# A short clear and a wait for it behind every state gather of the four layers

## The reference

```
h = jnp.maximum(_layernorm(x, axis=-1), 0.0);  x = x + L0(h, src, dst, edge_type)
h = jnp.maximum(_layernorm(x, axis=-1), 0.0);  x = x + L1(h, edge_index)
h = jnp.maximum(_layernorm(x, axis=-1), 0.0);  x = x + L2(h, src, dst)
h = jnp.maximum(_layernorm(x, axis=-1), 0.0);  x = x + L3(h, edge_index)

L0:  m = sum over r of mask[etypes == r] * (feat[src] @ weight[r]);  segment_sum(m, dst)
L1:  three times   h = segment_sum(h[src], dst) / max(cnt, 1) @ Wl + h @ Wr + b   (relu between)
L2:  f = feat * rsqrt(out_deg);  s = segment_sum(f[src], dst);  t = segment_sum(f[src] * f[dst], dst)
     (s @ weight1 + t @ weight2) * rsqrt(in_deg)
L3:  two graph attention layers (4 heads of 32, then 1 head of 64): softmax over each dst's edges
```

## Time and profile before

| | before |
|---|---|
| median of 3 runs | 6565.89 us (6560.53 to 6572.52) |
| profiled execution: its span (its own time is given by no other number) | 8635.1 us |
| mean granted TensorE clock in the profiled execution | 0.650 |
| GpSimd busy, share of the span | 4305.3 us, 50% |
| VectorE busy | 4326.1 us, 50% |
| TensorE busy (multiplications) | 4016.2 us, 47% |
| ScalarE busy | 2282.2 us, 26% |

### The profile page before, as it was taken

How to read it: one execution, slowest core, us unless ns; L and a number is a source line. 1 busy time by engine, 2 the same in 40 slices (tenths; PEclk the granted TensorE clock), 3 DMA queues, 4 the chain that set the end, 5 groups by cost and what they waited for, 6 DMA issues and landing times. The chain is left out here.

```text
span 8635.1 us, 76490 instructions
## 1 busy us (share of the span) xinstructions
PE 4016.2 (47%) x19708; PEld 2671.9 (31%) x19708; DVE 4326.1 (50%) x14882; ACT 2282.2 (26%) x5999; POOL 4305.3 (50%) x4026
## 2 busy tenths in 40 slices
PE   1111158312888825654563664342465476567000
PEld 0000034101555514443442443332344355233000
DVE  3010069301999944434432553565244698677553
ACT  0000000001777621110110333354111133799000
POOL 5777720575000046546555674774555100888577
PEclk8555589655999955555555555555666666798555
DMA  1111100000222222222222343343122144555222
GB/s 42 47 46 47 47 19 0 21 1 5 103 113 107 99 70 79 69 73 64 69 68 63 112 128 112 94 139 112 44 68 68 77 161 163 125 146 138 76 82 77
DMA packets 413612, 684.96 MB, mean 79 GB/s; under 512 B 283685, under 2 KB 290444, under 8 KB 407978
## 3 DMA queue, kind: packets, MB, share of 16 engines
q1 hardware_dynamic: 282410, 542.14, 17.7%
q0 software_dynamic: 130944, 140.05, 7.5%
HBM read 310.94 MB, written 373.78 MB: 79 GB/s over the span
## 5 line engine op out<-in xcount | busy, mean ns | idle before, releaser
L711 POOL DMA_INDIRECT G<-states,srcq x1568 | 1678.9, 1071 | 851.1 <-issue 479.5
L1133 DVE TENSOR_TENSOR_SCAN R<-same,R,G 128x28 f32<-128x28 f32 x4480 | 883.8, 265 | 622.1 <-issue 499.9
L1793 PE MATMUL PS<-ident,HH 128*128 128x128 f32 x2357 | 529.8, 376 | 1257.4 <-ACT AT L2063 373.2
L2063 ACT COPY AT<-PS 128x512 f32<-128x512 f32 (+1 forms) x494 | 283.7, 581 | 2467.3 <-remote 1375.1
L1793 PEld LDWEIGHTS PS<-ident,HH 128*128 128x128 f32 x2357 | 402.8, 205 | 1332.9 <-issue 409.9
L711 POOL DMA_INDIRECT EE<-node_info,srcq x392 | 394.4, 1006 | 545.0 <-DMA node_info<-XC 415.7
L1701 PE MATMUL PS<-R 128*128 128x392 f16 x784 | 283.0, 361 | 673.2 <-remote 375.7
L711 POOL DMA_INDIRECT G<-states,srci x392 | 406.7, 1038 | 321.0 <-ACT HH L2161 199.1
L1808 PEld LDWEIGHTS PS<-WD,AT 128*128 128x128 f32 x2358 | 505.8, 316 | 183.0 <-issue 182.7
L1808 PE MATMUL PS<-WD,AT 128*128 128x64 f32 x2358 | 560.6, 416 | 0.0
L824 POOL DMA_INDIRECT out_nodes<-O,dstq x392 | 430.9, 1099 | 188.2 <-issue 123.3
(11 more groups left out here) (412 smaller groups left out, 10157.6 us busy)
## 6 DMA issues: line engine op xcount, KB each, us to landing
states<-O SPq DMA_DIRECT2D x70, 896.0 KB, 3.6
HH<-states SPq DMA_DIRECT2D x56, 896.0 KB
total<-R SPq DMA_DIRECT2D x56, 896.0 KB
XB<-resid SPq DMA_DIRECT2D x42, 896.0 KB
states<-HH SPq DMA_DIRECT2D x28, 896.0 KB, 3.9
G<-states,srcq POOLq DMA_INDIRECT x1568
resid<-XB SPq DMA_DIRECT2D x28, 896.0 KB
xl_of_src<-O SPq DMA_DIRECT2D x14, 1792.0 KB
```

Source lines behind the costliest of these rows:

```text
L711: return pool.indirect_dma_start(to, None, table_, bass.IndirectOffsetOnAxis(ap=idx, axis=0), bounds_check=bound, oob_is_err=False).then_i ...
L1133: last = dve.tensor_tensor_scan(out=out_[:, order, f], data0=flags[:, order], data1=in_[:, order, f], initial=initial[:, f:f + 1], op0=ALU ...
L1793: last = pe.transpose(PS[:, 4 + k, q * P:(q + 1) * P], HH[:, b, (g * G4 + q) * D2:(g * G4 + q + 1) * D2], ident[:])
L2063: act.copy(AT[:, k, 0:n * P], PS[:, 4 + k, 0:n * P]).then_inc(s_copied, 1)
```

## The change

A tile `idle` of 64 columns is added, which nothing reads. Behind each gather of a layer GpSimd clears it (`memset`, 128 x 64 numbers) as a `step`: it waits for the end of the clear before it goes on. There are 4 x 14 x 28 = 1568 such pairs. The other phases' gathers stay as they were, and so do the waits for `chunk_scanned`.

```diff
@@ -148,6 +148,7 @@
         fw = sb("fw", [P, 2, 6, HCOLS])
+        idle = sb("idle", [P, 64])
@@ -713,6 +714,9 @@
+            def pause():
+                step(pool.memset(idle[:], 0.0))
+
             moved = 0
@@ -819,6 +823,8 @@
                     for j in range(C):
                         gather(G[:, b, j * D:(j + 1) * D], table_, idx[:, at + j:at + j + 1], table_.shape[0] - 1, s_g[b])
+                        if phase in LAYERS:
+                            pause()
```

## The result

The change makes the kernel slower: 7575.87 us (4 runs, 7573.41 to 7590.95) against 6564.61 us (now 4 runs of the kernel before), a ratio of 1.1548 with a 95% interval of 1.1532 to 1.1565, or 1011 us more. The forecast was 7050 us, 483 us more: the direction is right and the time lies inside the range, but the size is less than half of what came.

A forecast was written before the change was run, and what follows sets the result against it. In timed layers GpSimd's gathers nearly bound the kernel, with 5.4 us a chunk spare. 1568 x (0.90 + 0.50) = 2195 us for 1712 us, +483 us on 6566, gives 7050 us; range 6350 to 7730 us.

The forecast's parts named there:

- The clear: Layers, behind each gather: clearing 64 columns on GpSimd takes 0.14 us, about halfway between 0.10 and 0.19 us.
- The gap: Layers, from clear's end to next gather: 0.79 us, as the gather's preparation is not done ahead of a wait.
- The step in the profile's own terms: Layers, gather to gather in profiled time: from 1.30 to 1.93 us, by 0.63 us.
- how the profile stands to the timed runs: Whole kernel: timed runs are 2069.2 us shorter, all in the nine gather stretches; a timed gather takes 0.90 us.
- the ten other stretches: Outside the gather stretches: VectorE's or TensorE's own work, 2558.3 us, taken as equally long in timed runs.
- spare time: Layers, timed: GpSimd has 5.4 us a chunk beyond its gathers (30.6 - 25.2), which hides part of the pauses.
- The shortening of 0.63 to 0.50 us: Layers, cost per pause: 0.63 us scaled as the whole run by 0.76, 0.48 rounded up to 0.50 us.
- the forecast by itself: Whole kernel: the main case without its rivals, 7050 us, between 6750 and 7400 us; chance 0.50.
- the dear pause: Rival, layers: no preparation overlaps and no idle 0.30 us is replaced, 0.93 us a gather, 7723 us; chance 0.14.
- Relief: Rival, layers: holes of VectorE and ScalarE set the pace and spaced gathers close them; about 6400 us; chance 0.25.
- the rule cited against the forecast: Layers: two-input VectorE scans contend with GpSimd reading SBUF, not only writing it, so each clear gives VectorE an open port.
- the cheap pause: Rival, layers: the wait costs only 0.07 us, so 0.21 us a gather with the clear, 6594 us; chance 0.11.

The follow-up runs named there:

- the run with the lagging wait: Against the kernel before: clears behind all 1568 layer gathers, but GpSimd waits only for the clear before the last one (two spare tiles); 6627.59 us, ratio 1.011.
- the second profile: The kernel before, unchanged, profiled once more: 6551.6 us, ratio 0.9996, profile span 6562.4 us where the first profile's was 8635.1 us.

## Why the prediction was right and where it was wrong

- **The clear** was put at 0.14 us between two rows of other sizes; it took 0.172 us. 1568 x 0.032 = 50 us too little, a small miss.
- **The gap** was read as 0.79 us from the one released gather, as the preparation that no longer lies under its predecessor. It is 0.79 us behind almost every clear, and the run with the lagging wait and the one without a clear show the reason to be the right one: 936 of 1011 us go where the sequencer may run one gather ahead, and all of it where nothing stands behind the gather.
- **The step in the profile's own terms**, 1.93 us against 1.30, growing by 0.63 us, was right: 1.96 us and 0.647 us on average. 1568 x 0.63 = 988 us would have been the forecast by these rows alone.
- **The step that failed is the one on how the profile stands to the timed runs.** It took the ten other stretches as they are and put all 2069 us into the gathers, which made a timed gather step by 0.90 us, the layers' gather stretches 1712 us and their spare time 5.4 us a chunk. Measured: 1.30 us from gather to gather, well above the 0.977 us that it held for the upper end, 1.385 us on average with the long ones and the starts of chunks, 2160 us in the layers, and no spare time. Two terms of the sum came from it. The shortening of 0.63 to 0.50 us took off 1568 x 0.13 = 204 us. The spare time, 1712 - 1568 x 0.90 = 301 us, was not there either. 483 + 204 + 301 = 988 us; with 0.647 in place of 0.63 us it is 1014 us, which is the difference of the groups.
- **The range** held the measured time by luck: the forecast by itself ended at 7400 us, and the range goes on to 7730 us only for the dear pause, whose mechanism did not come.
- **What the rows said that was not heard:** in the longest stretch of the earlier trace rows VectorE was busy for 138.15 of 1095.50 us, and right behind it, in the earlier trace rows, for 400.41 of 417.60 us, with work that, as the second profile shows, can run beside the x gathers. The holes of 1.12 us before the scans and the 1012.3 us of waits that the records don't name were the same sign; neither stands in the second profile. Work that was free to go and didn't go is where the first profile's time went; a gather that steps by 1.30 us in every plain stretch was no candidate. The prediction named these holes as perhaps the recording's own, and still looked for the 2069 us in the gathers alone.
- **Relief** (0.25) fell with the second profile: holes that a pause might have closed are not there. The 64 scans take 11.86/64 = 0.19 us each beside running gathers, as much as the earlier trace rows has them without gathers, so the rule cited against the forecast had nothing to give to the scans. What got shorter are the gathers, by 35.7 us in all.
- **The dear pause** (0.14, 0.93 us) was too dear by the 0.30 us that the gap replaces; **the cheap pause** (0.07 us behind the clear) took a row whose follower is no DMA.
- Of the signs named beforehand, the clears, the gap, the step near 1.93 us and the end of waits for scans came as named; the layers' stretches are 788 to 799 us, a little over the 730 to 780 us.
- What made the other engines stand still in the first profile is open. No run here was made to bring it about.

## What to carry to other kernels

Here a wait in GpSimd's queue cost what the sequencer could have prepared during it: 0.49 us on a step of 1.30 for each gather that waits for an instruction right ahead of it, beside the clear's own 0.17, and nearly nothing where the wait lags by one. If a profile's span and the median of the runs differ by as much as here, the first thing to look for is a stretch in which an engine has work and doesn't do it; a step that reads the same in every stretch should not be scaled to close the sum. With an engine that is the bound, each added instruction can be priced from three rows: its own duration, the gap behind it, and the gap that it replaces.

## What the runs showed of the hardware

- GpSimd's sequencer runs far ahead of its indirect DMAs: 19 register moves in the time of 8 gathers. The lead grows to 12 gathers and stays: in the second profile of before the move of the first layer's 31st gather stands at 1749.3 us, right behind the end of the 18th (1748.26 + 1.00).
- Between two gathers lies a gap of 0.30 us in which a clear of 64 columns has nearly room: with the lagging wait it adds 75/1568 = 0.05 us a gather.
- Some gathers take 1.2 to 2.9 us in place of 1.00. In the second profile of before there are 102 of them among the layers' 1568, and each of the 102 overlaps one of VectorE's products of 128 x 1792 numbers (about 2 us); 55 others overlap one as well and take 1.00 us. One of the 102, with VectorE's product beside it:

```profile
1929.68 2.02 DVE L1295 TENSOR_TENSOR HH<-R,inv_in 128x1792 f32<-128x1792 f32 x1
...
1930.73 1.85 POOL L711 DMA_INDIRECT G<-states,srcq  x1 [0.30 <-issue]
```

The Trainium skill, SBUF — State Buffer, section "Who interferes with whom", names such a pair, a VectorE instruction with two SBUF inputs beside a GpSimd instruction that reads SBUF. The gather reads its row numbers from `srcq` in SBUF. Here the trace agrees for the products, at 0.3 to 1.9 us for each of the 102, by overlap alone, since no run takes the products away. The scans have two such inputs as well, but none of the 451 gathers that lay beside scans and no product took longer than 1.12 us.
